# Expert rows in place order in DRAM, half of each group's row transposes done by VectorE in 32 by 32 blocks

## The reference, cut to what matters

```
t = rmsnorm(layernorm(x)) * scale            # [T, 128]
vals, idx = top_k(t @ gate_w.T + gate_b, 4)  # 32 experts, 4 for each token
w = softmax(vals)
h1 = t @ w1[e].T + b1[e]                     # 256 wide: even columns glu, odd columns lin
glu, lin = min(h1[::2], 7), clip(h1[1::2], -7, 7)
h = glu * sigmoid(1.702 * glu) * (lin + 1)
out[token] = sum over its 4 experts of w * (h @ w2[e].T + b2[e])
x = x + 0.5 * (layernormed x + out)
attention:  q = softmax(.), k = softmax(.), ctx = (q k^T / row sum) v, 16 heads of 8
```

## Time and profile before

| | us |
|---|---|
| median of 3 runs | 726.69 (723.95 to 727.34) |
| the profiled execution, own time | 724.5 |
| its span in the trace | 722.8 |
| busy PE / DVE / ACT / POOL | 525.7 / 437.0 / 347.9 / 505.3 |

### The profile page before, as it was taken

One profiled execution on the slowest core, in us unless ns is written; L12 is line 12 of the kernel. 1 busy time (PEld: TensorE's weight loads), 2 busy tenths in 40 slices (PEclk: granted clock), 3 DMA queues, 4 the chain that ended last, 5 costly groups with the idle time before them and its releaser, 6 DMA issues.

```text
span 722.8 us, 12887 instructions
## 1 busy us (share of the span) xinstructions
PE 525.7 (73%) x3232; PEld 443.3 (61%) x3235; DVE 437.0 (60%) x1243; ACT 347.9 (48%) x752; POOL 505.3 (70%) x551
## 2 busy tenths in 40 slices
PE   6258887999999998395607864999999999834000
PEld 3154266999898997163504552699989999734000
DVE  7889223555457778388993877255555767744222
ACT  4444414666566665495607743366656666511000
POOL 3677777777437777777677777777752777777765
PEclk9557999999999999697558955999999999967555
DMA  7997115666556664221111111466655666424222
GB/s 267 390 382 287 54 52 166 199 198 197 177 164 196 199 197 154 64 55 53 48 51 55 51 52 54 137 199 208 203 183 161 197 199 204 153 72 126 65 63 57
DMA packets 56491, 108.26 MB, mean 150 GB/s; under 512 B 12576, under 2 KB 19968, under 8 KB 56320
## 3 DMA queue, kind: packets, MB, share of 16 engines
q1 hardware_dynamic: 40064, 74.13, 30.9%
q0 software_dynamic: 16384, 33.59, 16.1%
HBM read 51.00 MB, written 56.62 MB: 149 GB/s over the span
## 4 chain that ended last, share of the span: by engine, by line
PE 48%; POOL 17%; DVE 13%; issue 11%; ACT 6%; DMA 4%; POOLq 0%; DVEq 0%; ACTq 0%; SPq 0%
PE PS L1242 19%; PE PS L1137 11%; PE PS L1255 10%; POOL xs L535 10%; POOL YG L560 6%; ACT swish L668 3%; PE PS L1356 2%; DMA xrow<-xs 2%; DVE PS L986 1%; DMA xs<-U,row 1%; DMA YG<-ys,row 1%; PE PS L1342 1%; DVE st L717 1%; PE PS L1317 1%; DVE chosen L777 1%
## 5 line engine op out<-in xcount | busy, mean ns | idle before, releaser
L560 POOL DMA_INDIRECT YG<-ys,row x256 | 245.5, 959 | 117.7 <-issue 77.5
L535 POOL DMA_INDIRECT xs<-U,row x256 | 249.4, 974 | 81.9 <-issue 73.2
L1242 PE MATMUL PS<-W,xT 128*128 x768 | 183.1, 381 | 0.2 <-DVE glulin L931 0.2
L1242 PEld LDWEIGHTS PS<-W,xT 128*128 128x128 f32 x768 | 139.0, 191 | 16.1 <-issue 0.9
L931 DVE TENSOR_SCALAR glulin<-PS 128x512 f32<-128x512 f32 x96 | 66.4, 691 | 127.8 <-PE PS L1255 100.0
L625 ACT ACTIVATE yrow<-PS 128x512 f32<-128x512 f32 x96 | 57.3, 597 | 108.7 <-PE PS L1255 108.7
L1255 PEld LDWEIGHTS PS<-W,hidT 128*128 128x128 f32 x768 | 99.9, 191 | 14.4 <-issue 10.0
L1255 PE MATMUL PS<-W,hidT 128*128 x768 | 102.3, 276 | 7.0 <-ACT hidT L633 6.9
L944 DVE SCALAR_TENSOR_TENSOR hid<-glulin,swish 128x512 f32<-128x512 f32 x96 | 66.7, 694 | 15.9 <-ACT swish L629 15.2
L637 ACT ACTIVATE xT<-PS 128x512 f32<-128x512 f32 x96 | 56.5, 589 | 38.8 <-PE PS L1137 38.8
L629 ACT ACTIVATE swish<-glulin 128x512 f32<-128x512 f32 x96 | 60.5, 630 | 22.3 <-DVE glulin L931 14.1
(11 more groups left out here) (178 smaller groups left out, 710.3 us busy)
## 6 DMA issues: line engine op xcount, KB each, us to landing
xrow<-xs SPq DMA_DIRECT2D x96, 256.0 KB
ys<-yrow SPq DMA_DIRECT2D x96, 256.0 KB, 2.2
xs<-YG SPq DMA_DIRECT2D x6, 2048.0 KB, 13.4
W<-in_w12T SPq DMA_DIRECT2D x1, 6144.0 KB
xs<-U,row POOLq DMA_INDIRECT x256
YG<-ys,row POOLq DMA_INDIRECT x256
out<-X SPq DMA_DIRECT2D x7, 256.0 KB, 2.5
X<-in_x SPq DMA_DIRECT2D x4, 256.0 KB, 3.7
```

The costliest lines, as they stand in the source:

```text
L535: pool.indirect_dma_start(out=xs[c], out_offset=bass.IndirectOffsetOnAxis(ap=row[:, i:i + 1], axis=0), in_=U[:, (c * CT + t) * H:(c * CT + ...
L560: pool.indirect_dma_start(out=YG[:, t * TOPK + k, :], out_offset=None, in_=ys[c], in_offset=bass.IndirectOffsetOnAxis(ap=row[:, i:i + 1], ...
L1242: last = te.matmul(h1, xT[:, s, q * P:(q + 1) * P], W[:, bass.ds(es[q], 2 * H)], start=True, stop=True)
```

## The change

Rows lie in xs and ys in the order of their places, so the place is the row number and the four instructions of `slots_to_rows` go, nine times. A load for a group now takes the two first tiles by one DMA with 512-byte runs (two to a partition), and the other two tiles by four DMAs of 32 partitions each, which read runs of 128 bytes: the DMA for columns 32j to 32j+31 brings 32-by-32 blocks so that after VectorE has transposed every block in place (one `transpose` of 128x256 to PSUM, `turn_blocks`) the two tiles stand transposed. PE transposes only the two first tiles. For group 0 of each chunk one DMA brings all four tiles and PE transposes all of them. Stores to ys write runs of 512 bytes, four to a partition, where before a partition's 2048 bytes went in one run. There are two new semaphores: `blocks_loaded` (the four DMAs) and `blocks_turned` (VectorE's transpose), for which ACT's copy to xT and SP's block loads of two groups later wait. The constant matmuls ahead of layer 0's experts go from 18 to 38.

```diff
-NIDLE_E = (18, 34)
+SQ = 32
+TURNED = 2
+NIDLE_E = (38, 34)
...
-        xs_v = [a.rearrange("(g p q) h -> g p (q h)", p=P, q=GT) for a in xs]
-        ys_v = [a.rearrange("(g p q) h -> g p (q h)", p=P, q=GT) for a in ys]
+        xs_v = [a.rearrange("(g n) h -> g n h", n=GT * P) for a in xs]
+        ys_v = [a.rearrange("(g q p) h -> g p q h", p=P, q=GT) for a in ys]
...
                     wait_count(sp, turned, k + (t0 - 4 if c == 0 and isinstance(k, int) and k < 2 else t0 - 1))
-                    sp.dma_start(xrow[:, r, :], xs_v[c][bass.ds(k, 1)].rearrange("g p n -> (g p) n"))\
-                        .then_inc(xrow_loaded[r], 16)
+                    rows = xs_v[c][bass.ds(k, 1)].rearrange("g n h -> (g n) h")
+                    first = isinstance(k, int) and k == 0
+                    n = GT if first else GT - TURNED
+                    if first and c:
+                        sp.wait_ge(blocks_turned, f * (NGF - 2) + NG - 2)
+                    sp.dma_start(xrow[:, r, 0:n * H].rearrange("p (q h) -> p q h", h=H),
+                                 rows[0:n * P].rearrange("(q p) h -> p q h", p=P)).then_inc(xrow_loaded[r], 16)
+                    if not first:
+                        if isinstance(k, int) and k == 1 and c:
+                            sp.wait_ge(blocks_turned, f * (NGF - 2) + NG - 1)
+                        elif not isinstance(k, int) or k >= 2:
+                            wait_count(sp, blocks_turned, k + (f * (NGF - 2) + c * (NG - 1) - 2))
+                        for j in range(P // SQ):
+                            cols = slice(j * SQ, (j + 1) * SQ)
+                            sp.dma_start(xrow[cols, r, n * H:GW].rearrange("a (i b) -> a i b", b=SQ),
+                                         rows[n * P:GT * P, cols].rearrange("(i a) b -> a i b", a=SQ))\
+                                .then_inc(blocks_loaded[r], 16)
...
                         act.wait_ge(turned, k + (t0 + 1))
+                        wait_count(act, blocks_turned, k + (f * (NGF - 2) - second))
                         wait_count(act, multiplied, k + (m0 - 1))
...
+                    def turn_blocks(n, b, m, second):
+
+                        before = f * (NGF // 2 - 2) - second if b == 0 else f * (NGF // 2) + 1
+                        dve.wait_ge(blocks_loaded[b], (m + before) * (16 * P // SQ))
+                        dve.wait_ge(turned, n + (t0 + 1))
+                        cols = slice((GT - TURNED) * H, GW)
+                        v.transpose(TP[b][:, cols], xrow[:, b, cols]).then_inc(blocks_turned, 1)
...
+                    if live(k, -1, NGF) and not (isinstance(k, int) and (k + 1) % NG == 0):
+                        turn_blocks(k + 1, s, m + r, second)
                     add(1)
...
-                def slots_to_rows(first, stop):
-
-                    pr = slice(first * TOPK, stop * TOPK)
-                    linked[0] += 1
-                    v.tensor_scalar(pos_a[:, pr], pos[:, pr], P - 1, None, ALU.bitwise_and).then_inc(chain, 1)
-                    link(v.tensor_scalar(pos_b[:, pr], pos[:, pr], 7, GT - 1, ALU.logical_shift_right, ALU.bitwise_and))
-                    link(v.scalar_tensor_tensor(pos_a[:, pr], pos_a[:, pr], float(GT - 1), pos[:, pr], ALU.mult, ALU.add))
-                    v.scalar_tensor_tensor(row[:, c * PAIRS + first * TOPK:c * PAIRS + stop * TOPK], pos_b[:, pr],
-                                           float(1 - P), pos_a[:, pr], ALU.mult, ALU.add).then_inc(rows_ready, stop - first)
...
-                    last = turn(TP[r], xrow[:, r, :], GT)
+                    alone = isinstance(k, int) and k % NG == 0
+                    last = turn(TP[r], xrow[:, r, :], GT if alone else GT - TURNED)
```

More of the change, by code:

```diff
@@ L253, in build @@
         xrow_loaded = [sem(f"xrow_loaded{r}") for r in range(2)]
+        blocks_loaded = [sem(f"blocks_loaded{r}") for r in range(2)]
         turned = sem("turned")
+        blocks_turned = sem("blocks_turned")
         xT_ready = sem("xT_ready")
@@ L617, in experts, with step @@
                 g0, t0, m0 = f * NGF, f * (NGF + 3), f * (NGF + 3)
-                def step(k, r, m):
+                def step(k, r, m, second=0):
                     s = 1 - r
@@ L635, in step, with step_of_second @@
                         act.wait_ge(turned, k + (t0 + 1))
+                        wait_count(act, blocks_turned, k + (f * (NGF - 2) - second))
                         wait_count(act, multiplied, k + (m0 - 1))
                         a.activation(xT[:, r, :], TP[r], ACT.Copy, bias=1.0).then_inc(xT_ready, 1)
-                sweep(act, 8, NGF, 4, step, steps=4)
+                def step_of_second(k, r, m):
+                    step(k, r, m, second=1)
+                sweep(act, 8, NGF, 4, step, cut=NG, late=step_of_second, steps=4)
             def attention(c, n):
@@ L848, in end @@
                     v.tensor_scalar(ended[:], slot_no[:], span[:, 0:1], None, ALU.is_ge).then_inc(ended_ready, 1)
-                def rows(first, stop):
-                    slots(first, stop)
-                    slots_to_rows(first, stop)
                 if c == NCHUNK - 1:
@@ L857, in route @@
                     tile_experts()
-                    rows(0, GT)
+                    slots(0, GT)
                 elif ph == 0:
                     begins(0, 1)
-                    rows(0, 1)
+                    slots(0, 1)
                     begins(1, CT)
-                    rows(1, GT)
+                    slots(1, GT)
                     end()
@@ L881, in weights @@
                                                 ALU.mult, ALU.mult))
-                return slots, slots_to_rows, weights
+                return slots, weights
             def split(src, rest, dst):
@@ L917, in experts, with step @@
                 g0, t0, m0 = f * NGF, f * (NGF + 3), f * (NGF + 3)
-                def step(k, r, adding=None):
+                def step(k, r, m, second=0, adding=None):
                     s = 1 - r
@@ L953, in experts, with four @@
                 for k in range(4):
-                    step(k, k % 2)
-                with dve.Fori(0, (COMB_A - 4) // 4) as i:
+                    step(k, k % 2, k // 2)
+                with dve.Fori(0, (NG - 8) // 4) as i:
                     for j in range(4):
-                        step(i * 4 + (4 + j), j % 2)
-                with dve.Fori(0, CTA // 2) as i:
+                        step(i * 4 + (4 + j), j % 2, i * 2 + (4 + j) // 2)
+                for k in range(NG - 4, COMB_A):
+                    step(k, k % 2, k // 2, second=int(k >= NG))
+                def four(i):
                     for j in range(4):
-                        step(i * 4 + (COMB_A + j), j % 2, Combine(i * 2 + j // 2, j // 2, i, 0, f) if j % 2 else None)
+                        step(i * 4 + (COMB_A + j), j % 2, i * 2 + (COMB_A + j) // 2, second=1,
+                             adding=Combine(i * 2 + j // 2, j // 2, i, 0, f) if j % 2 else None)
+                with dve.Fori(0, CTA // 2 - 1) as i:
+                    four(i)
+                four(CTA // 2 - 1)
                 for k in range(COMB_A + 2 * CTA, NGF + 1):
-                    step(k, k % 2)
+                    step(k, k % 2, k // 2, second=1)
             def combine(ph, first, stop):
@@ L1114, in _ @@
             attention(0, NCHUNK)
-            slots, slots_to_rows, weights = route(NCHUNK, NCHUNK + 1, lambda: combine(NCHUNK - 1, CTB, CTB + 6))
+            slots, weights = route(NCHUNK, NCHUNK + 1, lambda: combine(NCHUNK - 1, CTB, CTB + 6))
             slots(GT, CT)
-            slots_to_rows(GT, CT)
             weights()
```

17 lines of the change are left out of this document (7 added, 10 removed).

## The result

The changed kernel takes 737.1 us (median of 6 runs, 735.55 to 738.55) and the kernel before 725.45 us beside it (723.48 to 727.34): ratio 1.015, 95% interval 1.0126 to 1.0174. It is slower by 11.7 us. The forecast was no change (727.5, with a range of its own of 725 to 730), and the time lies outside that. It lies inside the whole range (722.5 to 741), and of the cases it is nearest to rival B.

A forecast was written before the change was run, and what follows sets the result against it. It took POOL's chain of indirect DMAs to bind. Change of chunk +2.8 and gather 1 -2.0 gave +0.8 us: 725.3 for a profiled run, 727.5 as median (726.69 + 0.8); range 722.5 to 741.

The forecast's parts named there:

- rival B: Expert loop: SP's six issues and 1792 short runs push a group past 3.49 us; +13 us, 739.5; chance 0.26.
- What bounds the kernel: Whole kernel: POOL's chain of indirect DMAs, 1.26 us from start to start, binds; a faster PE only buys idle PE time.
- SP per group: SP's queue in the expert loop: four block loads, load, store and branch cost 3.2 us a group, bounds 2.9 and 3.5.
- POOL's waits for the experts' progress: Sign on POOL that the forecast is wrong: `keep_to_experts` waits appear, meaning a group time over 3.49 us.
- the block transposes' waits for the blocks: Sign on VectorE that the forecast is wrong: block transposes wait for `blocks_loaded`; no size given.
- The 1024 short runs: DMA queues, per group: 128-byte runs take 1.15 us on 16 engines, within a sum of 2.9 to 3.2, up to 3.7.
- The row order at 0: Rows in place order: row numbers worth 0; only 0.3 us later landing of 512-byte-run stores at each change of chunk.
- VectorE: Expert groups: a block transpose takes 0.42 us (bounds 0.2 and 0.7), making 3.0 us a group, under PE's 3.27.
- The 20 matmuls: Ahead of layer 0's experts: they end about when the first load lands, first group at full clock; 0, bounds 0 and +0.5.
- The change of chunk: Between chunks 0 and 1: PE idles about 5 us awaiting scatters, its clock falls; +1.4 us, twice, +2.8.
- rival A: At the change of chunk the clock holds: -0.1 us each, sum -2.3, 724.4; chance 0.17.
- Gather 1: POOL ahead of gather 1 in each layer: its late start goes, -1.2 and -0.8, together -2.0 us.

The follow-up runs named there:

- e4: The kernel before with two of the four row transposes of each group left out and nothing in their place; 860.58 us against 864.08, ratio 0.998.
- e5b: The changed kernel with SP's group loops written out, so addresses and waited counts are constants, at full speed; 732.55 us against 726.06 before, ratio 1.010.
- e2: The changed kernel with a group's 1024 runs of 128 bytes issued by one DMA instead of four; 863.19 us against 864.08 before, ratio 0.999.
- e3: The changed kernel with four block DMAs of 32 runs of 1 KB each instead of 256 of 128 bytes; 872.27 us against 864.08 before, ratio 1.0105.
- e9: The changed kernel with its blocks loaded by eight DMAs instead of four, same 1024 runs of 128 bytes; 907.08 us against 726.06 before, ratio 1.249.
- e10: The kernel before with only the new row order, PE turning all four tiles, 18 idle matmuls, at full speed; 730.07 us against 726.06, ratio 1.006.
- e12: The kernel before with the new row order, PE turning all tiles, 38 idle matmuls and SP's loops written out; 730.87 us against 726.06, ratio 1.006.
- a1: The changed kernel as it stands, rerun as control at the slower speed; 874.58 us against 861.89 for the kernel before, ratio 1.013.

## Why the prediction was wrong

That 737.1 us lies inside the stated range says little for the forecast: the range was wide enough to hold rival B.

**What bounds the kernel: right.** POOL's chain binds, and 20 us less of PE work are worth next to nothing. e4 shows it at the slower speed; at full speed e5b had PE waiting for the scatters at both changes of chunk (1.81 and 4.48 us) while most of POOL's starts stayed 1.26 us apart.

**SP per group: the step that failed.** "I take 0.48" was right for a block issue (0.49), and 0.2 us a group for the loop's branch was right too (0.61 instead of 0.20 behind the store, once in two groups). The term that was too small in "a group costs 4 x 0.48 + 1.10 + about 0.2 for the loop's branch = 3.2 us (bounds 2.9 and 3.5)" is the 1.10 for load and store: with the time between issues they take 0.39 + 0.29 + 0.27 + 0.41 + 0.20 = 1.56 us in the step from 156.28. So a group costs SP 3.5 to 3.8 us, at or beyond the upper bound, 3.65 in the mean of the two kinds of step, which is the group time at which rival B was priced. The 1.10 came from the earlier trace rows, where 0.54 us lie between the starts of store and load; it took the rest, the time from load back to store, as wait for yrow and so as free. Part of it is SP's own register work. The forecast thereby fell and rival B came out, by one of its two mechanisms, SP's issues, and with two of the signs that were named for it: POOL's waits for the experts' progress and the block transposes' waits for the blocks. That its 739.5 us are only 2.4 above the median of 737.1 is in part luck. It had 6.3 to 6.5 us for each layer; gathers 1 and 3 were late by 4.5 and 13.6, which is 4.5 for the first layer and 9.1 for the second, and the row order, which B didn't count, is worth 4.6 by itself. The mean group over the four chunks is 3.57, 3.59, 3.49 and 3.77 us (23 steps each, first to last W1 start) against 3.41, 3.52, 3.40 and 3.49 before.

**The 1024 short runs: not what sets the group time, as forecast.** Against the Trainium skill ("DMA: Bandwidth & Descriptors", section "Specifications"), whose rule on transfers under 512 bytes spoke for B: the trace does not agree that the short runs set the time here. e2 (short runs, one issue) recovered, e3 (long runs, four issues) did not, and e9 lost 25% with runs of the same size and number. This is shown at the slower speed for e2 and e3. At full speed e9 shows it, and e5b, where VectorE no longer waits for the blocks. That the short runs cost nothing at all at full speed isn't shown: e2 was not run there, and e5b is still 0.4% above the row order alone.

**The row order at 0: wrong by +4.6 us** (the spans of e10 and before; 4.0 by the medians). The prediction gave 0.3 us of landing for each of two stores and nothing else. e10 and e12 have it at 0.6%, of the change's 1.5%. The size is shown; the mechanism stays open.

**VectorE: right.** A block transpose took 0.458 us (0.42 estimated), and with it VectorE is 58.5 of 70 us busy at most (e5b in the window of gather 0).

**The 20 matmuls: worth nothing, as forecast, but not by the forecast's reason.** It had layer 0's first group run at full clock behind them. In the changed kernel the 38 matmuls end at 111.0, PE waits 1.92 us, and the granted clock is 0.50 all the same from 114.8 to 118.1, 2.3 us later than before; the first W1 takes 3.40 us (2.83 before).

```profile
114.80:118.10 3.30, 3.30 (x11) 2.57 (x10) 0.78 (x2) 1.88 (x2) 2.38 (x4) 0.50 0.70 163
```

**The change of chunk: not seen after, right where SP is relieved.** The forecast had PE idle for 5 us and the clock near 0.5. In the changed kernel PE was never early, as the groups of chunks 0 and 2 took 3.57 and 3.49 us in the mean (3.41 and 3.40 before): the load that waits for the scatters arrived while it was still busy. PE at the first change, as in the earlier trace rows:

```profile
196.43 1.99 PE L1266 MATMUL PS<-W,xT 128*128 x8
198.25 0.60 PE L1160 MATMUL PS<-ident,hid 128*128 128x128 f32 x4
198.69 0.60 PE L1160 MATMUL PS<-ident,xrow 128*128 128x128 f32 x4
```

No idle time stands in brackets, and the clock held. In e5b, with most groups at 3.3 to 3.4 us, one of two changes had the forecast's mechanism: 4.48 us idle, clock 0.50. It cost +3.0 us for the gather, twice the 1.4 forecast and at its bound of 3. The other went as rival A said: 1.81 us idle, clock kept, +1.0. This is seen in one execution.

**Gather 1: wrong sign after, right in e5b.** Forecast -1.2 and -0.8; after it was +1.6 and +1.9, as the groups of chunk 1 of each layer were late. In e5b the two are -1.2 and -0.8 to the tenth.

**A place that the prediction didn't name.** In the sixth step of chunk 1 VectorE waits for the first gathered rows with glu behind it. Before, it waits 2.27 us in layer 0 and 1.56 in layer 1, and PE 0.72 and under 0.1. In the changed kernel it is 3.05 and 3.68, and PE 2.35 and 2.84. Its layer 1 (the window is the stretch at the low clock):

```profile
569.61 0.35 DVE L915 SCALAR_TENSOR_TENSOR X<-YG,wtop,X  x1 [3.68 <-DMA YG<-ys,row]
...
571.86 1.83 PE L1279 MATMUL PS<-W,hidT 128*128 x8 [2.84 <-ACT hidT L650]
```

```profile
572.20:575.50 3.30, 3.30 (x16) 3.21 (x15) 1.86 (x5) 1.65 (x3) 2.69 (x3) 0.50 0.57 103
```

PE stands 2.84 us, the granted clock is 0.50 for 3.3 us behind it, and that step takes 7.64 us (3.85 before). In layer 0 the clock held. e5b has the same fall in layer 0 (PE idle 2.61 us, the clock 0.50 from 219.5 to 222.8, the step 7.64 us again). It is part of gather 3's lateness. That it follows from the gather starting later against the chunk beside it is argued, not shown. The rows alone (e10) already lengthen the step to 5.0 us in both layers (4.48 and 3.84 before).

How the 1.5% divides at full speed: about 0.6% is the row order (1.006), and writing out SP's loops took 1.015 to 1.010, so about 0.5% is SP's time between issues. These two intervals overlap a little (1.0126 to 1.0174 and 1.0061 to 1.0141); the single times don't (735.55 to 738.55 and 731.46 to 735.12), though they are from two sets. The remaining 0.4% (1.010 against 1.006) is at the edge of the intervals, and its cause isn't shown. Candidates are the two falls of the clock in e5b's trace and the short runs in the DMA queues, which no run took out at full speed. No version beat the kernel before at full speed.

## What to carry to other kernels

Count the instructions of a queue's engine, not its DMAs: an issue in a loop costs its DMA instruction, and the register work and branch around it, which is easily taken for waiting in a trace of a half-idle queue. A price for it must come from a stretch where the engine doesn't wait. And when an edit frees the engine that doesn't bind and loads the one that feeds it, the best case is nothing and only the feeder's term has to be exact.

## What the runs showed of the hardware

- From start to start a block load took SP about 0.5 us with register addresses (0.49) or with constant ones (0.50 to 0.54), and whether it carried 128 or 256 runs (3.99 / 8 and 1.95 / 4). In the loop 334 ns of it are the DMA instruction and the rest two register instructions with their gaps; written out there are none, and the DMA instruction takes 464 ns. What written-out loops save is the time between issues of different kinds and at the loop's end (0.2 to 0.6 us against 0.04 to 0.05).
- With four issues each, 1024 runs of 128 bytes gave 1.013 (a1, 1.0061 to 1.0200) and 128 runs of 1 KB 1.0105 (e3, 1.0074 to 1.0136): no difference outside the intervals. This is at the slower speed.
- VectorE's transpose of 128x256 fp32 in 32 by 32 blocks from SBUF to PSUM took 458 ns, a copy of that shape 424.
- Idle time of PE in an expert stage does not always cost the clock: 1.81 us (e5b) and 2.35 us (after, layer 0) left it at 1.00; 2.61 us (e5b) and 2.84 us (after, layer 1) brought 0.50 for some 3.3 us after work returned, and 4.48 us (e5b) for some 6.7 us.
- The same kernel before took 864, 862 and 726 us in three sets, and a row order that cost 0.6% at 726 cost nothing at 864 (0.997).
